# Pooled input made a block ahead on chip, block 0's scores in four banks, and two expert units inside the routing, in a one-core attention and mixture-of-experts kernel

## The reference

```python
# pooled input: one mask kind per sequence (l <= j, l >= j, l != j)
scores = tanh(x @ W1 + b1) @ v                        # one number per token
p = softmax(where(mask, scores, -1e30)); pooled = (p @ x) / count
# attention over each sequence, 16 heads of 8, a rotary part of 32 shared by the heads
c_kv = pooled @ W_kv_down
k, v = c_kv @ W_k_up, c_kv @ W_v_up;  k_rope = rotary(c_kv @ W_k_rope)
q = pooled @ W_q;  q_rope = rotary(pooled @ W_q_rope)
w = softmax(causal((q k^T + q_rope k_rope^T) / sqrt(40)))
x2 = x + (w v) @ W_o
# one of 64 matrices per sequence, then 64 experts, 8 of them per token
c = x2 @ W[cat] + b[cat]
s = sigmoid(c @ gate.T); sc = s + bias
# sum of the best two of each of 8 groups; the best 4 groups; in these the best 8 experts
weights = 2.5 * s[best 8] / sum(s[best 8])
out = x2 + sum_e weights_e * (silu(c @ Wg_e) * (c @ Wu_e)) @ Wd_e + shared expert
```

## Time and profile before

| what | value |
|---|---|
| median of 3 runs (lowest to highest) | 748.22 us (747.62 to 749.47) |
| the profiled execution | 748.22 us |
| its span | 746.4 us |
| PE busy | 721.3 us, 97% |
| DVE busy | 549.0 us, 74% |
| ACT busy | 453.5 us, 61% |
| POOL busy | 425.1 us, 57% |
| chain that ended last | PE 73%, DVE 11%, ACT 10% |

### The profile page before, as it was taken

One profiled execution on the slowest core, in us unless ns is written; L12 is line 12 of the kernel. 1 busy time (PEld: TensorE's weight loads), 2 busy tenths in 40 slices (PEclk: granted clock), 3 DMA queues, 4 the chain that ended last, 5 costly groups with the idle time before them and its releaser, 6 DMA issues.

```text
span 746.4 us, 15904 instructions
## 1 busy us (share of the span) xinstructions
PE 721.3 (97%) x5680; PEld 560.0 (75%) x5680; DVE 549.0 (74%) x1150; ACT 453.5 (61%) x873; POOL 425.1 (57%) x349
## 2 busy tenths in 40 slices
PE   8877999999999999999999999999999999999997
PEld 6765776677777777777787777777777777887885
DVE  5796668886698756976778766987668766886664
ACT  3755865477556675567555774566754675555553
POOL 2528667566456545655555654666446564566665
PEclk9999999999999999999999999999999999999999
DMA  7495443435534453444564344443634345345441
GB/s 264 141 356 135 123 121 99 127 94 156 120 107 118 123 144 109 129 103 127 125 117 134 98 150 113 120 113 120 141 113 135 103 125 128 102 125 141 128 134 46
DMA packets 69055, 97.21 MB, mean 130 GB/s; under 512 B 8016, under 2 KB 26896, under 8 KB 68976
## 3 DMA queue, kind: packets, MB, share of 16 engines
q1 hardware_dynamic: 64512, 91.21, 44.1%
q10 hardware_dynamic: 4464, 4.98, 1.9%
HBM read 90.73 MB, written 4.98 MB: 128 GB/s over the span
## 4 chain that ended last, share of the span: by engine, by line
PE 73%; DVE 11%; ACT 10%; issue 3%; POOL 2%; POOLq 0%; DVEq 0%; ACTq 0%
PE U L967 20%; PE Y L967 20%; PE G L967 19%; PE A L967 12%; DVE act_w L938 3%; POOL hid_lo L631 2%; ACT s_t L395 2%; ACT hid_hi L532 2%; DVE hid L950 2%; ACT L520 1%; ACT L395 1%; DVE k_blk L678 1%; ACT G L520 1%; PE A L1031 1%; DVE spread_p L861 1%
## 5 line engine op out<-in xcount | busy, mean ns | idle before, releaser
L631 POOL TENSOR_TENSOR hid_lo<-hid,hid_hi 128x512 fp32r<-128x512 f32 (+1 forms) x264 | 342.1, 1296 | 275.1 <-ACT hid_hi L532 274.0
L938 DVE TENSOR_TENSOR act_w<-G,cwb 128x512 f32<-128x512 f32 x248 | 170.4, 687 | 100.3 <-ACT G L520 99.3
L520 ACT ACTIVATE G<-G 128x512 f32<-128x512 f32 x248 | 144.4, 582 | 140.6 <-PE G L967 137.7
L532 ACT CAST hid_hi<-hid 128x512 fp32r<-128x512 f32 (+1 forms) x264 | 162.4, 615 | 71.8 <-DVE hid L950 70.5
L950 DVE TENSOR_TENSOR hid<-act_w,U 128x512 f32<-128x512 f32 (+1 forms) x256 | 175.8, 687 | 24.1 <-PE Y L967 1.5
L967 PE MATMUL Y<-hid_hi,wd_hi 128*128 128x512 f32 (+1 forms) x264 | 107.0, 405 | 5.4 <-POOL hid_lo L631 5.1
L967 PE MATMUL G<-c_hi,wg_hi 128*128 128x512 f32 x248 | 111.8, 451 | 0.2 <-DVE act_w L938 0.2
L967 PE MATMUL Y<-hid_hi,wd_lo 128*128 128x512 f32 (+1 forms) x264 | 103.6, 393 | 0.0
L967 PE MATMUL Y<-hid_lo,wd_hi 128*128 128x512 f32 (+1 forms) x264 | 103.4, 392 | 0.0
L967 PE MATMUL U<-c_hi,wu_hi 128*128 128x512 f32 x248 | 99.0, 399 | 1.1 <-DVE hid L950 1.1
L967 PE MATMUL G<-c_lo,wg_hi 128*128 128x512 f32 x248 | 97.5, 393 | 0.0
(11 more groups left out here) (191 smaller groups left out, 900.0 us busy)
## 6 DMA issues: line engine op xcount, KB each, us to landing
cwb<-cw_scratch SPq DMA_DIRECT2D x256, 256.0 KB, 3.7
k_blk<-in_cond_w SPq DMA_DIRECT2D x112, 64.0 KB, 2.4
wg_raw<-in_we_gate SPq DMA_DIRECT2D x8, 256.0 KB, 6.0
wu_raw<-in_we_up SPq DMA_DIRECT2D x8, 256.0 KB, 6.2
wd_raw<-in_we_down SPq DMA_DIRECT2D x8, 256.0 KB, 6.6
xf<-in_x_feat SPq DMA_DIRECT2D x8, 256.0 KB, 4.2
out_feat<-y ACTq DMA_DIRECT2D x8, 256.0 KB, 3.6
h_feat<-pooled_scratch SPq DMA_DIRECT2D x7, 256.0 KB, 2.7
```

The source lines that it names most:

```text
L520: nc.scalar.activation(gate_bank(p)[:, :], gate_bank(p)[:, :], ACT.Silu).then_inc(S["silu_done"], 1)
L532: nc.scalar.copy(hid_hi[0:n, p % NH, :], hid[0:n, p % NH, :]).then_inc(S["hi_ready"], 1)
L631: nc.gpsimd.tensor_sub(hid_lo[0:n, p % NH, :], hid[0:n, p % NH, :], hid_hi[0:n, p % NH, :].bitcast(F32)).then_inc(S["lo_ready"], 1)
L938: nc.vector.tensor_mul(act_w[:, p % NH, :], gate_bank(p)[:, :], cwb[:, p % NCW, :])\
```

## The change

Nine things are changed together.

- Pooled input. Only the pooled inputs of blocks 0 and 1 are made at the start. That of block b + 1 is made during block b's attention steps, for b from 1 to 6: its tokens are loaded into `xf` after the residual sum, DVE transposes a quarter of its probabilities ahead of each attention tile (`spread_part`), PE multiplies behind the gate product, and ACT copies to `h_feat` (step 23). The way through DRAM is gone.
- Scores of blocks 1 to 7. `q_grp` becomes one unmasked copy `q_sb`. A score product takes only the 32 rows of one group, and two groups alternate, into the banks A2 and A1; `s_t` is laid out by group instead of by tile. So turned probabilities wait for all four exponentials.
- Scores of block 0 keep the old form, but the four tiles go to four banks one after the other. Two of the four key masks are made on ACT from a second key product in bank G1.
- Turned probabilities of block 0 alternate between two banks.
- The pool weights of the second group come before block 0's attention sums; the third group's scores, weights and hidden product come later.
- Block 1's first products are issued between block 0's output product and gate product. Units 0 and 1 of block 0 issue their gate and up products during block 0's routing (`rotate(1)`, `rest_of_input(0, 0)` and the queries and keys of block 1 come before it). Their routing weights don't go through DRAM: PE spreads them with a selecting matrix `pick` (`first_weights`), and the DRAM loads begin with unit 2.
- Splits. 10 are made before unit 0; 15 in units 9 to 23.
- Loads. Three weights are asked for on ACT's queue; the category matrices of block 0 go to unused rows of `wd_raw`, earlier on SP; the later weights wait for block 0's category product.
- Fewer `warm` products; the eight banks become one tensor, so PE's rows say `banks`.

The diff, cut to what the prediction speaks of:

```diff
-        BEFORE_UNITS = 17
-        SPLIT_UNITS = range(11, 11 + NSPLIT + 1 - BEFORE_UNITS)
+        BEFORE_UNITS = 10
...
-        WARM = {9: 4, 12: 2, 13: 2, 14: 2, 15: 2, 21: 24}
+        WARM = {12: 1, 13: 1, 14: 1, 15: 1}
...
-                            sp.wait_ge(S[f"h_stored{i}"], 16)
+                elif p == 21 and 0 < blk < NBLK - 1:
+                    sp.wait_ge(S["x2_ready"], blk + 1)
                     sp.sem_inc(S["load_turn"], 1)
-                    sp.dma_start(h_feat[:, :], h_dram[:, bass.ds(blk * TOK + TOK, TOK)]).then_inc(S["h_in"], 16)
+                    token_load(blk + 1, "xt_in")
...
+            def key_masks(heads, blk):
+                act.wait_ge(S["k_again_ps" if opening(blk) else "k_ps"], 1 if opening(blk) else blk + 1)
+                wait(act, "score_tile_ps", blk * TILES)
+                for h in heads:
+                    nc.scalar.mul(k_blk[:, h, :], (G[1] if opening(blk) else A1)[:, :], C["head_of_group"][:, h:h + 1]).then_inc(S["k_ready"], 1)
+            def pooled_out(i):
+                act.wait_ge(S["pooled_ps"], i + 1)
+                if i == 1:
+                    act.wait_ge(S["v_ps"], 1)
+                elif i >= 2:
+                    act.wait_ge(S["wo_ps"], i)
+                nc.scalar.copy(h_feat[:, :], (A0 if i == 0 else G[1] if i == 1 else A1)[:, :]).then_inc(S["pooled_ready"], 1)
...
                     if p == 1:
                         act.wait_ge(S["q_ps"], blk + 1)
-                    nc.scalar.mul(q_grp[:, p - 1, :], A2[:, :], C["group"][:, p - 1:p]).then_inc(S["q_ready"], 1)
+                        if opening(blk):
+                            for g in range(NG):
+                                last = nc.scalar.mul(q_first[:, g, :], A2[:, :], C["group"][:, g:g + 1])
+                        else:
+                            last = nc.scalar.copy(q_sb[:, :], A2[:, :])
+                        last.then_inc(S["q_ready"], 1)
+                        if blk < 2:
+                            key_masks((range(2, HG), range(HG))[blk], blk)
...
-                if not prev and p in SPLIT_UNITS:
-                    split(BEFORE_UNITS + p - SPLIT_UNITS[0])
-                if p == 0 and not prev:
-                    pooled_out(7)
-                if p == X2_MOVED and not prev:
-                    act.wait_ge(S["h_stored6"], 16)
+                if not prev and BEFORE_UNITS <= p + 1 <= NSPLIT:
+                    split(p + 1)
...
+            rope_add(1)
             pool.wait_ge(S["cw_ready"], 1)
-            for i in range(7, 10):
-                split(i)
-            rope_add(1)
-            for i in range(10, BEFORE_UNITS):
+            for i in range(7, BEFORE_UNITS):
                 split(i)
...
                     t = p - 13
+                    if 0 < blk < NBLK - 1:
+                        spread_part(blk + 1, t)
                     ps = (A0, A2)[t % 2][:, 0:HEADS * VC].rearrange("p (h m) -> p h m", m=VC)
...
+            def spread_part(i, s):
+                if i >= 1 and s == 0:
+                    dve.wait_ge(S["pooled_ps"], i)
+                rows = slice(SEQ * s, SEQ * s + SEQ)
+                nc.vector.transpose(pool_pt[rows, :, s, :], pool_p[rows, bass.ts(i, TILES), :]).then_inc(S["pool_spread"], 1)
...
             for p in range(UNITS):
                 attention_half_step(p, 0)
                 attention_step(p, 0)
-                if p == 13:
-                    pool_scores(2)
+                if p == 9:
+                    pool_weights(1)
                 elif p == 16:
-                    pool_weights(1)
                     spread(1)
                 elif p == 18:
-                    spread(2)
-                    pool_weights(2)
+                    pool_scores(2)
                 elif p == 20:
-                    spread(3)
-                    spread(4)
...
-            spread(5)
-            rotate(1)
-            spread(6)
-            for i in range(1, 5):
-                dve.wait_ge(S[f"h_stored{i}"], 16)
-            for p in range(AHEAD):
-                attention_step(p, 1)
-            spread(7)
+                    rotate(1)
+                    rest_of_input(0, 0)
+            attention_step(0, 1)
+            attention_step(5, 1)
...
-                    dve.wait_ge(cwb_in[p % NCW], b * (16 * NPAIR // NCW) + 16 * (p // NCW + 1))
-                    nc.vector.tensor_mul(act_w[:, p % NH, :], gate_bank(p)[:, :], cwb[:, p % NCW, :])\
+                    if b == 0 and p < 2:
+                        dve.wait_ge(S["cwb_ps"], p + 1)
+                        gate, weight = act_w[:, p, :], G[p]
+                    else:
+                        loaded = b * NPAIR // NCW + p // NCW + 1 - (1 if p % NCW < 2 else 0)
+                        dve.wait_ge(cwb_in[p % NCW], 16 * loaded)
+                        gate, weight = gate_bank(p)[:, :], cwb[:, p % NCW, :]
+                    nc.vector.tensor_mul(act_w[:, p % NH, :], gate, weight)\
...
+                    pool_weights(2)
+                if not prev and p == 0:
+                    now = []
                 for step, blk in now:
...
                 wait(pe, "cwT_ready", blk)
                 mm(A0[:, :], rope_w[:, :], h_feat[:, :]).then_inc(S["rope_ps"], 1)
                 mm(A2[:, :], W["q"], h_feat[:, :]).then_inc(S["q_ps"], 1)
                 mm(A1[:, :], k_w[:, :], h_feat[:, :]).then_inc(S["k_ps"], 1)
+                if opening(blk):
+                    mm(G[1][:, :], k_w[:, :], h_feat[:, :]).then_inc(S["k_again_ps"], 1)
...
+                elif p == 6 and opening(blk):
+                    pe.wait_ge(S["rope_mask_ready"], 1)
+                    pe.wait_ge(S["k_ready"], HG)
+                    pe.wait_ge(S["tanh_done"], 2)
+                    for t in range(TILES):
                         for g in range(NG):
                             for r in range(SPT):
                                 tok = bass.ts(t * SPT + r, SEQ)
-                                last = mm((A2, A1)[t % 2][32 * r:32 * r + 32, bass.ts(g, P)], q_grp[:, g, tok], k_blk[:, :, tok])
+                                last = mm(first_scores[t][32 * r:32 * r + 32, bass.ts(g, P)], q_first[:, g, tok], k_blk[:, :, tok])
                         last.then_inc(S["score_tile_ps"], 1)
+                elif p in (6, 8) and not opening(blk):
+                    pair = (p - 6, p - 5)
+                    if p == 6:
+                        pe.wait_ge(S["rope_mask_ready"], blk + 1)
+                        pe.wait_ge(S["k_ready"], blk * HG + HG)
+                    else:
+                        pe.wait_ge(S["biased_tile"], blk * NG + 2)
+                    for s in range(SPB):
+                        t, r = divmod(s, SPT)
+                        for g in pair:
+                            rows = slice(32 * g, 32 * g + 32)
+                            last = mm((A2, A1)[g % 2][32 * r:32 * r + 32, bass.ts(t, P)], q_sb[rows, bass.ts(s, SEQ)],
+                                      k_blk[rows, :, bass.ts(s, SEQ)], tile_position=(32 * g, 32 * r))
+                    last.then_inc(S["score_tile_ps"], 2)
...
+                    if 0 < blk < NBLK - 1:
+                        pool_out(blk + 1)
...
-                if p == CWT:
-                    warm(8)
+            for p in range(CWT):
                 attention_step(p, 0)
...
-                    mm(Y[:, 0:NSEQ], cat_table, onehot).then_inc(S["cat_ps"], 1)
+                    mm(Y[:, P:2 * P], cat_table, onehot).then_inc(S["cat_ps"], 1)
                 elif p == 18:
                     pool_out(1)
-                elif p == 20:
-                    pool_out(2)
+                elif p == 19:
+                    pe.wait_ge(S["pooled_ready"], 2)
+                    mm(G[0][:, :], rope_w[:, :], h_feat[:, :]).then_inc(S["rope_ps"], 1)
                 elif p == 21:
-                    pool_out(3)
-                    pool_out(4)
+                    mm(A1[:, :], k_w[:, :], h_feat[:, :]).then_inc(S["k_ps"], 1)
+                    pe.wait_ge(S["tanh_gate"], 1)
+                    mm(A2[:, :], W["q"], h_feat[:, :]).then_inc(S["q_ps"], 1)
                 if p >= 9:
-                    warm(WARM.get(p, 0))
-            first_products(1)
-            pool_out(5)
-            pool_out(6)
-            for p in range(AHEAD):
-                attention_step(p, 1)
+                    warm(WARM.get(p, 0), Y)
+            def first_weights():
+                pe.wait_ge(S["cat_read"], 1)
+                warm(9, Y)
+                attention_step(CWT, 0)
+                pe.wait_ge(S["cwT_ready"], 1)
+                pe.wait_ge(S["silu_done"], 2)
+                pe.wait_ge(S["pick_ready"], 1)
+                for u in range(2):
+                    dst = G[u].rearrange("p (u two n) -> p two u n", two=2, n=P)
+                    for i in range(2):
+                        last = mm(dst[:, i], pick[:, u, i, :], cw_feat[:, :])
+                    last.then_inc(S["cwb_ps"], 1)
...
+                if not prev and p == 0:
```

(6 more changed lines are left out.)

300 lines of the change are left out of this document (141 added, 159 removed).

## The result

Median of four runs of the changed kernel, 739.88 us (736.98 to 741.32), beside 747.92 us before: ratio 0.9882, 95% interval 0.9858 to 0.9906. A second set, taken later beside the experiments, gave 740.62 us (739.62 to 740.76) and 0.9893 (0.9872 to 0.9915). Faster was right, by 1.1%; the forecast of 730.1 us was 10 us too low.

The account below looks back on a forecast made before the run. PE bounds steady blocks, a latency chain the start: 748.2 - 17.7 (start to unit 6) - 9.2 (score pairs) + 5.3 (pooled products) + 3.5 (splits) = 730.1 us. Forecast's own range 725 to 735; ends 723 and 741.

Parts of the forecast that it names:

- Block 0 up to its routing weights: Start of the kernel: routing weights ready near 49.4 instead of 56.21, 6.8 us earlier (bounds 4 and 8.5).
- From the routing weights to unit 6: Start, behind block 0's routing: unit 6 at about 66.3 instead of 83.95, 17.7 us earlier in all (bounds 13 and 20.5).
- Unit 6 behind 71: Sign of being wrong: unit 6's gate product, forecast near 66 us, issued later than 71 us.
- Case D: At the start a split, the keys' load or ACT's queue is late, only 6.8 us stay, 10.9 lost: 741; chance 0.06.
- Splits: Weight splits on POOL in block 0's units meet block 1's routing on DVE: 3.5 us added (bounds 0 and 7.5).
- Score pairs: PE's score products of blocks 1 to 7: 1.05 us a pair instead of 1.89, 9.2 us off in all.
- B: Score products: two groups of rows don't work side by side, the 9.2 us gain is gone: 739; chance 0.20.
- E: Score products: the small tiles follow each other, a pair takes 1.7 us above 1.89, slower than before: 763; chance 0.05.
- nine tenths through: Share of twelve score pairs' 10.1 us saving let through, as PE may newly wait on other engines: 9.2 us off.
- A steady block near 86.1: Sign of being right: the length of a steady block in us; over 87 would be a sign of being wrong.
- Pooled products: Six blocks' pooled inputs made behind the gate product on PE, 0.88 us each: 5.3 us added (bounds 4.8 and 6.3).
- C: The POOL and DVE lock strikes at each of seven routing instructions, 7.5 us instead of 3.5: 734; chance 0.14.

## Why the prediction was wrong, step by step

**Block 0 up to its routing weights: right, a little optimistic.** Ready at 51.25, not 49.4: the first routing instruction took 1.36 instead of 0.29 beside POOL, which was named, and the routing began 0.8 later.

**From the routing weights to unit 6: the step that failed, 7.2 us.** Unit 6 behind 71 was one of the prediction's own signs of being wrong; it came at 73.46. "The turn and its copy take 0.8, so the stores go at about 50.3." They went at 55.99, of which 1.85 came from the step before and 3.9 from what stands ahead of the turn on PE's queue: a wait for the rotary keys that are loaded behind twelve other loads, and nine warming products. Case D had "the keys' load" among the late things, at 0.06, but the row of SP's queue was never put beside PE's. Neither costs anything by itself: with the keys early the warming products lie in idle time, and without the products the keys' wait ends when the weights are ready. So the two single edits each move the turn to 51, and their gains at the turn don't add up. The store's way back was shorter than forecast (58.94 to 62.45, 3.5 and not 5.0). Then 11.0 instead of 8.1 from landing to unit 6: the half clock, 2.8 by the kernel that keeps it up, and 1.6 in the changed kernel's second profile. The prediction weighed the half clock at the first score tile, where it did not come back, and not behind the new idle time.

**Unit 6 to unit 10: a cost set at nothing.** The pooling weights of the third group were not priced in block 0's units at all. They cost 3.5 us, shown by moving them: 2.6 of their own DVE time in front of unit 7's weighting, and the half clock that PE's wait for it brought in the executions profiled.

**Splits: right mechanism, size too large.** The term was 3.5 us added. Units 18 to 27 took 23.51 us instead of 22.34 before, so 1.2 was added; the early splits give 1.7 back, as the kernel before paid for some of it already. Block 1's routing did meet them on DVE. One instruction of it in the changed kernel, in block 0's units and in a steady block:

```profile
125.66 1.10 DVE L791 TENSOR_SCALAR rt<-rt 128x32 f32<-128x32 f32 x1
```

```profile
299.94 0.17 DVE L791 TENSOR_SCALAR rt<-rt 128x32 f32<-128x32 f32 x1
```

Five such instructions (0.73 to 1.27 each between 118.80 and 128.24) lost some 3.8 us of DVE's time against their shortest, and 1.7 of it came through to PE. What covered the rest wasn't tried. Not all of it is the splits' doing: one of the five, with 1.27 at 118.80, is as long in a steady block, where POOL has no splits, and another (0.89 at 121.84) took 1.30 with the splits early:

```profile
294.33 1.28 DVE L754 TENSOR_TENSOR rt<-rt 128x32 f32<-128x32 f32 x1
```

```profile
124.55 1.30 DVE L779 TENSOR_TENSOR rt<-rt 128x32 f32<-128x32 f32 x1
```

The first of these two is from the changed kernel, the second from the one with early splits. So the earlier trace rows gave a pair of values for one instruction, and which value an instruction gets isn't set by the splits alone.

**Score pairs: right price, wrong share.** 1.08 a pair against 1.05 forecast, and two groups of rows do work side by side, so B and E fall. But "nine tenths through" was two thirds: two pairs save 1.62 us a block, the pooled product takes 0.90 back, and of the 0.72 left only 0.18 arrived, because the new layout needs both banks at once. That is shown: with the wait moved to the banks' reading another 0.57 came through. Over the blocks from the second on this is the 2.8 us missing in the last line of the first table. (Twelve pairs at 0.84 and nine tenths are 9.1, not 9.2; that changes nothing.) "A steady block near 86.1" was a weak sign: from rotary product to rotary product blocks took 86.30 to 86.97 before and 86.25 to 86.55 now.

**Pooled products: right.** 1.11 with its tail; units 10 to 18, where the first one stands, took 23.20 us instead of 22.30, so 0.90 against 0.88 forecast. None of PE's three idle times over 0.2 us in the steady block (0.56 at the second pair, 0.24 at a transpose, 0.46 at a product) is for their load or copy, and the last two stood there before (0.25 and 0.46).

**The cases.** The time came out near D's 741 only in part by D's mechanism: the keys' load was late, as D has it, but the early units were done at 46.5, well ahead of the routing's end, and 10.5 us of the start arrived where D left 6.8; the rest was lost in three other places. That the sum hits D's number is chance. C, 4 us more for the splits, did not happen. With the found causes taken away the kernel takes 728.3, near the 730.1 of the sum. That doesn't confirm the sum: misses of both signs are in it, and the early splits and the weaker wait take away what the sum had counted as lost.

Still open: how much of each single edit reaches the end. For the keys' load, the pooling weights and the splits the traces show 2.5 to 4.3, 3.5 and 1.7 us, the medians 2.2 to 2.9, 2.0 to 2.7 and 1.2 (the first two less by the ratios), and no run tells whether the start's variation from one execution to the next is the whole reason. Nor is it shown why PE's clock falls behind one short wait and not behind another of the same length.

## What to carry to other kernels

When a chain of latencies is shortened, list for its last link everything that stands ahead on its engine's queue, loads and filler included, each with its own source and its own place in its queue; what was hidden before is exposed first there. When work is laid out so that one instruction group touches more buffers at once, the wait ahead of it grows to the last of them: wait for the reading of the buffer, not for what is computed from it. And price short work by the point at which its engine stands when it comes, not by the engine's load over a block.
